# Making the high part of a batch's features on GpSimd instead of ScalarE, in front of the first sweep of a batch norm

## The reference

```python
def _L1(x):                            # two graph convolutions, then four LSTMs over windows
    h = relu(adj @ (x @ Wg0 + bg0)); h = relu(adj @ (h @ Wg1 + bg1))
    for p in range(1, 5):              # windows of p nodes, the last state replaces the last node
        last = lstm_last(Wih[p-1], Whh[p-1], ..., windows(h, p))
        h = h.at[:, arange(nw) * p + (p - 1), :].set(last)
    return h

def _L2(features):                     # A_hat: normed adjacency
    agg = einsum('nm,bmd->bnd', A_hat, features)
    h = relu(batchnorm(agg.reshape(-1, d) @ W1.T + b1, g1, be1))
    return batchnorm(h @ W2.T + b2, g2, be2)

x = layernorm(x + _L1(x))
x = layernorm(x + _L2(x))
```

## Time and profile before

| What | us |
|---|---|
| median of three runs | 995.13 |
| lowest and highest of them | 993.33, 995.75 |
| the profiled execution, its own time | 996.82 |
| its span in the profile | 994.9 |
| mean granted clock of PE over the span | 0.983 |

### The profile page before, as it was taken

The page is one execution under the profiler, slowest core; times in us unless marked ns, Lnnn a source line. Parts: engine busy times, 40 slices in busy tenths (PEclk is TensorE's granted clock), DMA queues, the critical chain, the costliest instruction groups (busy, mean ns, idle before and its releaser), DMA issues. The chain is left out here.

```text
span 994.9 us, 14572 instructions
## 1 busy us (share of the span) xinstructions
PE 933.1 (94%) x5202; PEld 801.6 (81%) x5202; DVE 664.6 (67%) x1628; ACT 546.2 (55%) x1136; POOL 311.3 (31%) x289
## 2 busy tenths in 40 slices
PE   7999998999999999999999999899989999978993
PEld 5689987899998898998889899788778974556773
DVE  7665444445647657665755775598887877788867
ACT  2042314764636565554656564557677648475667
POOL 3011222331233234223323333224333230155663
PEclk9999999999999999999999999999999999999998
DMA  8040011001010100101010010301010000000014
GB/s 227 2 82 22 2 43 64 22 22 43 1 44 1 43 22 1 43 2 43 1 43 22 3 42 1 125 1 56 14 39 22 1 1 1 0 1 1 1 43 127
DMA packets 33994, 31.62 MB, mean 32 GB/s; under 512 B 8450, under 2 KB 28034, under 8 KB 33924
## 3 DMA queue, kind: packets, MB, share of 16 engines
q1 hardware_dynamic: 32900, 30.64, 10.0%
q10 hardware_dynamic: 960, 0.07, 0.1%
q0 software_dynamic: 64, 0.00, 0.0%
HBM read 22.83 MB, written 7.87 MB: 31 GB/s over the span
## 5 line engine op out<-in xcount | busy, mean ns | idle before, releaser
L1368 ACT ACTIVATE gates<-psum,gbias 128x256 f32<-128x256 f32 (+2 forms) x312 | 159.2, 565 | 70.5 <-PE psum L67 66.1
L65 PE MATMUL psum<-LS,WI 128*128 128x256 f32 (+2 forms) x312 | 104.1, 334 | 8.8 <-ACT gates L1368 6.2
L78 POOL TENSOR_TENSOR LS<-A,LS 128x512 fp32r<-128x512 f32 (+2 forms) x44 | 48.6, 1105 | 177.5 <-ACT LS L1353 177.4
L67 PE MATMUL psum<-LS,WI 128*128 128x256 f32 (+2 forms) x312 | 102.9, 330 | 0.0
L66 PE MATMUL psum<-LS,WI 128*128 128x256 f32 (+2 forms) x312 | 102.9, 330 | 0.0
L78 POOL TENSOR_TENSOR LS<-Hodd,LS 128x512 fp32r<-128x512 f32 (+2 forms) x44 | 48.3, 1097 | 153.2 <-ACT LS L1353 153.2
L78 DVE TENSOR_TENSOR yl<-psum,yh 128x512 fp32r<-128x512 f32 x58 | 39.6, 689 | 65.5 <-ACT yh L1310 43.9
L78 POOL TENSOR_TENSOR XSl<-X,XSh 128x512 fp32r<-128x512 f32 x32 | 43.0, 1344 | 107.0 <-ACT XSh L1305 107.0
L65 PE MATMUL psum<-B2h,LT2h 128*128 128x256 f32 x256 | 72.7, 284 | 1.0 <-DVE X L1481 1.0
L65 PEld LDWEIGHTS psum<-LS,WI 128*128 128x128 f32 x312 | 59.2, 190 | 17.4 <-POOL LS L78 10.2
L67 PE MATMUL psum<-B2h,LT2l 128*128 128x256 f32 x256 | 72.4, 283 | 0.0
(11 more groups left out here) (379 smaller groups left out, 2699.8 us busy)
## 6 DMA issues: line engine op xcount, KB each, us to landing
WI<-lstm_weights SPq DMA_DIRECT2D x14, 512.0 KB, 3.6
WH<-lstm_weights SPq DMA_DIRECT2D x11, 512.0 KB, 4.6
X<-in_x SPq DMA_DIRECT2D x16, 256.0 KB
out<-X SPq DMA_DIRECT2D x16, 256.0 KB, 2.3
lstm_weights<-WI SPq DMA_DIRECT2D x4, 512.0 KB, 3.2
lstm_weights<-WH SPq DMA_DIRECT2D x3, 512.0 KB, 2.7
A<-in_adj SPq DMA_DIRECT2D x4, 256.0 KB, 4.4
z_A<-in_adj SPq DMA_DIRECT2D x1, 1024.0 KB, 5.3
```

The lines of the kernel that those rows point to most:

```text
L65: pe.matmul(out, lhs[0], rhs[0], start=start, stop=False)
L67: return pe.matmul(out, lhs[1], rhs[0], start=False, stop=stop)
L78: return eng.tensor_tensor(out, full, high.bitcast(F32), ALU.subtract)
L1368: act.activation(gates[:, gate, 0:n], sh.psum[:, gate, 0:n], ACT.Tanh if gate == G else ACT.Sigmoid, bias=gbias[:, p_ - 1, gate:gate + 1]) ...
```

## The change

ACT's `split_z` is removed with its entry in ACT's loop. Its waits and its copy, now a `tensor_copy`, stand at the head of POOL's `split_z`; POOL then waits for its own copy and makes the low part as before. The written order is not changed, so the copy takes the place in POOL's queue at which the low part stood.

```diff
@@ ACT @@
-            def split_z(n):
-                if n >= 2:
-                    act.wait_ge(S["ring_mm"], ring["a", n - 2] + 1)
-                else:
-                    powers_used(act)
-                    if n == 1:
-                        act.wait_ge(S["ah_lo"], C)
-                act.wait_ge(S["x2_done"], n + 1)
-                act.activation(bn["XZh"][:, n % 2, :, :], sh.X[:, :, n, :], ACT.Copy).then_inc(S["xz_hi"], 1)
...
-                elif kind == "xz":
-                    split_z(*at)
@@ POOL @@
             def split_z(n):
+                if n >= 2:
+                    pool.wait_ge(S["ring_mm"], ring["a", n - 2] + 1)
+                else:
+                    powers_used(pool)
+                    if n == 1:
+                        pool.wait_ge(S["ah_lo"], C)
+                pool.wait_ge(S["x2_done"], n + 1)
+                pool.tensor_copy(bn["XZh"][:, n % 2, :, :], sh.X[:, :, n, :]).then_inc(S["xz_hi"], 1)
                 pool.wait_ge(S["xz_hi"], n + 1)
                 low_part(pool, bn["XZl"][:, n % 2, :, :], sh.X[:, :, n, :], bn["XZh"][:, n % 2, :, :])\
                     .then_inc(S["xz_lo"], 1)
```

## The result

The changed kernel takes 998.08 us in the median of 20 runs (994.49 to 1000.52), the kernel before 995.20 us in 20 runs beside it (992.19 to 998.76). The ratio of the runs is 1.0025 with a 95% interval of 1.0015 to 1.0034: slower by 1.5 to 3.4 us. The profiled execution took 999.9 us with a span of 998.0.

A forecast was written before the change was run, and what follows sets the result against it. PE was taken to bound the touched stretch (busy 107.3 of 115 us). Terms of -1.6 + 1.3 + 1.8 = +1.5 us took the profiled 996.82 us to 998.3, or 996.6 as a median of runs; range 993.5 to 1000.5.

The forecast's parts named there:

- ACT's relief: At PE's waits ending at 706.28, 732.71 and 760.57: ACT's gates come 0.53 us earlier, 1.6 us less in all.
- The copy's price: On POOL, each of 16 copies of 128x512 takes 0.7 us plus 0.2 us waiting for itself, 14 us more together.
- The lock: A POOL instruction of length t holds a DVE operation in SBUF for t - 0.25: 0.45 us per copy, 1.1 per low part.
- The LSTM part: Up to 789, collisions of POOL with DVE change place: 0.7 us at batch 5 plus 0.6 elsewhere, 1.3 us more.
- The two more places: At batches 8 and 9 in the LSTM part, collisions like batch 5's, put at 0.3 us each.
- a step that I took for covered: Sign of being wrong: a PE wait appears at LSTM steps assumed to be covered; no size given.
- The end: At the sweep's end, from about 799, POOL's copies and low parts hold DVE's L584 runs: 0.7 to 2.8 us more.
- Both races: Low part against last L584 near 800 and 809, within 0.05 us: DVE loses 0.45 us or, if the low part is first, 1.5.
- term three: The loss at the end of the sweep, taken as the middle of 0.7 to 2.8 us: 1.8 us more.
- The first (POOL holds DVE longer): A copy near 1.34 us holds DVE 1.1 us instead of 0.45: +5.4 us, 1000.5; chance 0.28.
- The second (ACT's relief wins): DVE lets POOL's copy pass and a half-clock stretch after 732 may vanish (-1.7): -3.6 us, 991.5; chance 0.08 beyond 0.3%.
- The third: Losses and gains fall into PE's slack: -0.5 to +0.5 us, 995.1; chance 0.64 together with the forecast itself.

The follow-up runs named there:

- e4: The change without any high part for batches 2 to 11, and batches 0, 1 and 12 to 15 back on ACT; ratio 1.0003 to the kernel before.
- e2: The kernel before with only the high parts of batches 12 to 15 made by POOL; ratio 1.0038 to the kernel before.
- e3: The change, but POOL's copies of batches 12 and 14 wait until the norm of 13 and 15 is applied; ratio 0.9993 to the kernel before.
- e5: The kernel before plus a spare POOL copy of 128x512, feeding nothing, in each of batches 12 and 14; ratio 1.0036 to the kernel before.
- e6: The kernel before plus a spare POOL fill of 128x512 with zero in each of batches 12 and 14; ratio 1.0036 to the kernel before.
- e7: The change run again unaltered for a second profile; ratio 1.0025 to the kernel before.
- e1: The change with the high parts of batches 12 to 15 back on ACT, 0 to 11 on POOL; ratio 0.9988 to the kernel before.

## Why the prediction was right, point by point

Forecast: 0.15% slower, 993.5 to 1000.5 us, chances 0.64 for within 0.3% and 0.28 for slower. Measured: 0.25% slower, 998.08 us. The runs could tell that from no change, which I had put at 0.3%. The sum was +1.5 us; the sweep's two profiles give +1.3 and +1.8, and the runs 2.9 us between the medians. That the sum fits the sweep so closely is partly luck: the LSTM part came out 0.7 to 0.9 us better than its terms and the end 0.7 to 1.0 us worse, and the two misses cancel.

- **ACT's relief, -1.6 us at three waits of PE: right.** They shrank by 0.51, 0.39 and 0.51 us, 1.4 together, against 3 x 0.53. What I took for worth nothing elsewhere wasn't quite: PE's wait for `z_st` ahead of the aggregation near 695 (0.27 us in the kernel before) went too, and PE was 0.5 us further ahead behind it.
- **The copy's price, 0.7 us and 0.2 for POOL's own semaphore: nearly.** 0.62 us in the median and 0.08 us from its end to the low part's start. It is nearer to the writing-only form, as taken. The spare fill, which reads nothing, took 0.60 us too. By the Trainium skill (GPSIMD Engine Reference, section 4.1) one-input work runs at roughly line rate; the prediction's estimate of 0.43 us from it, without overhead, lies 0.19 us below the measured copy.
- **The lock: right, and shown.** The spare instructions and the copy kept away from L584 show it by itself. The rule of the Trainium skill (SBUF — State Buffer, "Who interferes with whom"), that a DVE instruction in a two-port mode and GpSimd exclude each other, makes no exception for a GpSimd instruction with one input; the trace agrees, if L584 runs in such a mode: the L584 that starts beside the copy of 798.82 takes 0.66 us instead of 0.35.

```profile
798.86 0.66 DVE L584 TENSOR_SCALAR X<-X,nscale,nshift 128x128 f32<-128x128 f32 x1
```

- **The LSTM part, +1.3 us against the relief: the term that was mis-sized.** Its sum with the relief was -0.3 and measured -1.0 to -1.2. Batch 5 came as worked out (PE's wait +0.64 us for 0.7 forecast). It was the first of the gate operations that was held, not the second, since the low part came earlier than drawn up: the copy, of 719.43, followed the POOL instruction ahead of it without a pause, and the low part stood 0.70 us behind the copy's start instead of 0.9. The two more places at 0.3 us each, of which I had no rows worked through, were +0.2 behind batch 9 and nothing behind batch 8; and a collision that went away, near 705, was worth 0.7 us against `e4` by 713 (1.2 us ahead against 0.55), a gain that I hadn't counted. A wait at a step that I took for covered appeared too, but a small one: 0.23 us for POOL's `LS` near 689 in the second profile of the change. The held gate operation of batch 5:

```profile
720.65 1.33 DVE L1648 TENSOR_TENSOR gates<-gates 128x512 f32<-128x512 f32 x1
```

- **The end, +0.7 to +2.8 us with the middle taken: the right place and mechanism, at the bad end.** +2.5 and +2.8. Both races were lost: an L584 that is drawn as starting just before the low part was held for its whole length, as here 0.08 us before the low part of 810.79:

```profile
810.71 1.45 DVE L584 TENSOR_SCALAR X<-X,nscale,nshift 128x128 f32<-128x128 f32 x1
```

With a gap of 0.08 us between copy and low part there was no race left to win, for the low part met the seventh L584, not the eighth. Had I worked with the gap that was measured, term three would have been 2.8 and the sum +2.5. Two details were wrong besides. The low part of batch 13 can hold DVE too: the second run's 4.47 us are 2.14, the 1.4 of batch 14's pair and 0.9 of batch 13's low part, which the forecast charged to PE alone. And the aggregation of batch 13 didn't wait for `z_XZl` in either profile of the change, only 0.13 us in `e2`; the 0.55 us put on it didn't come in that way.
- **The rivals.** The first (POOL holds DVE longer) gave the size at the end but for another reason; the copy was short. The second (ACT's relief wins) is the direction in which the sweep goes as soon as the four last batches stay on ACT, but by 1.1 us and not by 3.6; the half-clock stretch near 733 stayed in the change, and where it did vanish (`e3`) that was worth 0.7 to 0.9 us, not 1.7. The third is out: the interval leaves out no change.

**What stays open.** The sweep's 1.3 to 1.8 us lie at the lower edge of the interval of 1.5 to 3.4, so a good part of the runs' 2.9 us is not accounted for. The profiles can't supply it: the parts in which the kernels are alike vary by as much, the rest by 2.3 us and the stretch ahead of the sweep by 2.7 (the first matmul of batch 0's aggregation starts at 677.83 to 680.55, the two ends being one profile of the change and one of the kernel before). Whether the delays at the end of the sweep also make half-clock stretches likelier behind it, as the excess of the ratios of `e2`, `e5` and `e6` over their sweeps (1.2, 1.6 and 1.9 us: 3.8 less 2.6, 3.6 less 2.0, 3.6 less 1.7) might suggest, wasn't settled: the intervals are as wide as that, and the rest of these three profiles isn't longer than that of the kernel before again. The granted clock of the runs (each run's mean over its span, then the median) fits it: 0.982 in the 20 runs of the change, 0.982 in `e7` and `e6`, 0.983 in `e2` and `e5`, against 0.987 in the 30 and in the 19 runs of the kernel before beside the experiments, whose own two profiles, at 0.983, are not typical of it. But it is 0.983 in the 12 runs of `e1` as well, which is not slower.

## What to carry to other kernels

Moving work from ScalarE to GpSimd was paid for here not in GpSimd's own time but in VectorE's: look up what VectorE does in the microseconds in which the moved instruction will run, and above all whether the event that releases it is one in the middle of a run of VectorE's own copies or scalings. Where a semaphore of such a run releases GpSimd, wait for the end of the run; here that saved the 2.5 us again. And decide for each instance, not for the loop: in the profiles 12 of 16 moves gained 1.1 us together and 10 chosen ones 1.9 (2.8 with the clock that held), while all 16 were a loss.

## What the runs showed of the hardware that I had not expected

- A GpSimd fill of 128x512, which reads nothing, takes 0.60 us, as long as the copy (0.61), and holds a VectorE scaling in SBUF just as long: 0.64 us (0.66 beside the copy) for 0.35.
- The start that the profile draws doesn't tell who is held: the L584 drawn at 810.71, while the one ahead of it ran until 810.78, was held by a GpSimd instruction drawn at 810.79, until 812.16, where that one ended at 812.08.
- GpSimd's wait for its own copy took 0.08 us, a third of the 0.25 us that stood between its first two dependent instructions at the start of the program.
- A GpSimd copy in front can spare VectorE a collision: DVE's low part near 705 took 1.64 us without it and 0.98 with it.
